# Six sorted tiles of a graph layer are routed one or two steps later

## The reference, cut to what matters

```python
edge_index = jnp.stack([src, dst])
xn = _layernorm(x, axis=-1)
x = x + gnn(xn, edge_index, ...) + mix(xn[None], ...)[0]   # attention over edges; token mixing
x = x + ffn(_layernorm(x, axis=-1)[None], ...)[0]          # 8 experts, best 2 per node
```

## Time and profile before

| what | us |
|---|---|
| median of 3 runs (2192.88 to 2195.23) | 2193.44 |
| the profiled execution | 2191.56 |
| its span | 2189.8 |
| busy: PE, DVE, POOL, ACT | 1831.5, 1600.6, 1454.8, 1085.2 |

### The profile page before, as it was taken

One profiled execution on the slowest core, in us unless ns is written; L12 is line 12 of the kernel. 1 busy time (PEld: TensorE's weight loads), 2 busy tenths in 40 slices (PEclk: granted clock), 3 DMA queues, 4 the chain that ended last, 5 costly groups with the idle time before them and its releaser, 6 DMA issues. The chain is left out here.

```text
span 2189.8 us, 37617 instructions
## 1 busy us (share of the span) xinstructions
PE 1831.5 (84%) x9074; PEld 1332.9 (61%) x9075; DVE 1600.6 (73%) x3942; ACT 1085.2 (50%) x1932; POOL 1454.8 (66%) x1586
## 2 busy tenths in 40 slices
PE   8499998687777787775789999889999989997871
PEld 6367776566556565554566667667767777764540
DVE  7588887568677777697777888879878989731143
ACT  4333333236454555355556667667647767632210
POOL 3277777777777777775567777667777777700376
PEclk9799999888777877877999999999999999999985
DMA  9666565876666666655567777666778777622485
GB/s 331 140 191 180 170 173 147 263 218 193 167 176 175 182 175 184 177 143 152 161 186 208 210 207 217 190 179 192 194 195 210 213 208 181 166 68 70 145 248 161
DMA packets 287067, 402.19 MB, mean 184 GB/s; under 512 B 108915, under 2 KB 209555, under 8 KB 283262
## 3 DMA queue, kind: packets, MB, share of 16 engines
q0 software_dynamic: 74208, 206.08, 35.0%
q1 hardware_dynamic: 197036, 180.03, 27.5%
q10 hardware_dynamic: 15602, 13.59, 2.1%
HBM read 346.38 MB, written 82.48 MB: 196 GB/s over the span
## 5 line engine op out<-in xcount | busy, mean ns | idle before, releaser
L1546 POOL DMA_INDIRECT rows_g<-node_table,src_all x1347 | 1281.6, 951 | 506.5 <-issue 409.5
L2336 PE MATMUL psB<-rows_g,pick_e 128*128 128x260 f32 x2704 | 737.4, 433 | 138.7 <-issue 116.0
L2336 PEld LDWEIGHTS psB<-rows_g,pick_e 128*128 128x128 f32 x2704 | 576.6, 219 | 257.2 <-issue 155.0
L1721 DVE TENSOR_TENSOR rows_g<-rows_g,psD 128x2048 f32<-128x2048 f32 x169 | 384.9, 2277 | 0.0
L2134 ACT ACTIVATE pick_n<-local_row 128x1024 bf16<-128x1024 bf16 x169 | 178.6, 1057 | 214.1 <-PE psA L2325 203.5
L2377 PE MATMUL psC<-W_f,xnT 128*128 x448 | 225.8, 627 | 0.0
L1568 POOL DMA_INDIRECT rows_g<-set_dram,places x98 | 96.8, 988 | 168.5 <-issue 164.2
L1692 DVE TENSOR_TENSOR pick_e<-psD,slot_all 128x1024 f32<-128x1024 f32 x169 | 203.7, 1205 | 0.1
L2130 ACT ACTIVATE local_row<-local_row,minus_id 128x1024 bf16<-128x1024 bf16 x169 | 191.5, 1133 | 15.8 <-DVE both_f L2034 8.7
L1784 DVE COPY xn<-psD 128x256 f32<-128x256 f32 x112 | 47.2, 421 | 180.7 <-PE psD L2413 75.9
L2325 PEld LDWEIGHTS psA<-window,pick_n 128*128 128x128 bf16 x1352 | 54.2, 98 | 150.0 <-issue 145.5
(11 more groups left out here) (389 smaller groups left out, 3013.3 us busy)
## 6 DMA issues: line engine op xcount, KB each, us to landing
local_row<-local_dram SPq DMA_DIRECT2D x169, 256.0 KB
sent_dram<-sorted_dram SPq DMA_DIRECT2D x176, 128.0 KB
rows_g<-node_table,src_all POOLq DMA_INDIRECT x1347
xin<-sent_dram SPq DMA_DIRECT2D x112, 128.0 KB
set_dram<-xn SPq DMA_DIRECT2D x112, 128.0 KB
xnT<-in_xT_dram SPq DMA_DIRECT2D x96, 128.0 KB
acc<-node_table SPq DMA_DIRECT2D x49, 128.0 KB, 3.6
W_f<-in_x_dram SPq DMA_DIRECT2D x48, 128.0 KB, 2.9
```

What stands on the lines that cost most here:

```text
L1546: pool.indirect_dma_start(out=rows_g[:, r, j], out_offset=None, in_=node_table, in_offset=bass.IndirectOffsetOnAxis(ap=src_all[:, g, j:j + ...
L1721: dve.tensor_tensor(heads, heads, p_here.unsqueeze(3).broadcast_to([P, EG, HEADS, C]), ALU.mult).then_inc(ph_ready, 1)
L2336: last = pe.matmul(ps_sum[s % 2][:, 0:AW], pick_e[:, s % SLOTS, j], rows_g[:, s % RING, j, 0:AW], start=(j == 0), stop=(j == EG - 1))
```

## The change

```diff
         if t + 3 <= FULL:
-            at = max(at, route_at[t + 3] + (4 if t + 3 >= CUTS[0] else 5))
+            at = max(at, route_at[t + 3] + (4 if t + 3 >= CUTS[0] else 6))
+        if t + 2 < CUTS[0]:
+            at = max(at, route_at[t + 2] + 3)
```

## The result

Measured beside the kernel before, the changed kernel took 2166.32 us (median of 4 runs, 2165.59 to 2171.48) against 2193.16: the ratio is 0.9887, with a 95% interval of 0.9875 to 0.9899. That is 24.8 us less by the ratio and 26.8 by the medians. The prediction was 2173.8 us, 19.6 less. The span of the profiled execution went from 2189.8 to 2165.1 us.

A forecast was written before the change was run, and what follows sets the result against it. It took DVE's waits on PE's sorting product to hold up steps 82 to 89, and PE to bound steps from 94 on. -29.3 + 2 + 3.7 + 4 = -19.6 us gave 2173.8 us, range 2164 to 2182.

The forecast's parts named there:

- What bounds which steps: PE bounds steps 94 to 107; in steps 82 to 89 (112.9 us) neither PE nor DVE is always busy, something is serial.
- The five waits: DVE's waits on PE's sorting product in steps 82, 83, 84, 87 and 88, together 29.3 us, were to go.
- They are worth 29.3 us: Removing DVE's five waits on the sorting product was entered in the sum as 29.3 us less.
- (a) Step 82: DVE's `choose(21)` needs logits that PE forms late in step 81; 2 us given back, bounds 0 and 5.0.
- (b) Work moved past step 93: Three sorting-product halves of tiles 17 and 16 move to PE-bound steps 94 and 95; 3.7 us given back.
- (c) PE as the cover: In steps 82 to 93, without DVE's waits, steps must be long enough for PE; 4 us given back, at most 13.5.
- The clock rule: PE's clock dips thin out once long gaps go; the skill page would have them stay with the short gaps.
- All of it: Rival, chance 0.07: none of (a) to (c) shows in steps 82 to 93; 29.3 us less, 2160 to 2164 us.
- PE takes over: Rival, chance 0.18: DVE waits for PE's end of step instead; 7.1 us less, about 2186 us.
- The slower case: Rival, chance 0.05: PE falls to half clock for most of steps 82 to 93; at 0.65, 15 us slower, 2208 us.

The follow-up runs named there:

- e3: Kernel before with its own steps, plus four buffers of normalised rows for sorted tiles and three homes of the selection matrix; saved 14.1 us, ratio 0.9932.
- e2: Changed kernel with five instead of six steps behind the third tile ahead (routes 78, 80, 81, 83, 85, 86); saved 18.8 us, ratio 0.9914.
- e9: Kernel before with e3's buffers and only tile 21's route moved, from 77 to 78; saved 17.4 us, ratio 0.9926.
- e5: e3's buffers with e2's steps, against the kernel before; saved 28.0 us, ratio 0.9872.
- e1: Changed kernel without its rule of three steps behind the second tile ahead (routes 77, 81, 82, 83, 87, 88); saved 14.9 us, ratio 0.9923.
- e7: Kernel before with 46 extra unread PE products, in step 81 and at the start of steps 83, 84 and 88; ratio 1.0001.
- e6: Changed kernel with seven steps behind the third tile ahead instead of six, four behind the second instead of three; saved 7.4 us, ratio 0.9962.
- e12: Changed kernel with a ring of four buffers of normalised rows (`xd`) for every tile; ratio 0.9892.
- e4: Changed kernel with seven instead of six steps behind the third tile ahead; saved 28.1 us, ratio 0.9867.

## Why the prediction was right or wrong, point by point

**What bounds which steps.** Right. Steps 82 to 89 held the loss (112.9 us, now 90.5), and from step 94 on PE passes on what it gets (147.9 and 147.6 us for steps 94 to 107). Steps 82 to 93 take 133.8 us, within the 123 to 140 that were foretold.

**The five waits are gone.** Right: 29.3 us to 0.

**They are worth 29.3 us.** This step failed as a reason, and that its sum came out near is in part luck. By e3, taking away these waits and nothing else is worth 14.1 us, because PE's long steps then hold DVE up at the logits instead. The saving follows the fall of all of DVE's waits on PE in steps 80 to 93, whatever they wait for. From 31.3 us before they fall by 16.5 in e3, 19.1 in e2, 20.1 in e9, 23.3 in the change and 29.3 in e5, which save 14.1, 18.8, 17.4, 26.8 and 28.0; the match is loosest in e1, where they fall by 9.8 and 14.9 are saved. The prediction asked of each `normed` and `sort_out` where its product stood, but not how long PE's list was in that step, nor what else waited for its end. The change takes three things away together: the same-step waits (worth 9.2 us once nothing is three-deep, e5 against e2), the three-deep steps with ACT's wait for the store (13.9 us once there are no such waits, e5 against e3), and some half clock. Each masks part of the other: both alone come to 18.8 and 14.1, and together to 28.0, not 32.9. What the three-deep step, the store and the clock are worth each by itself stays open.

**(a) Step 82.** 2 us was put down; the wait on the logits of tile 21 is there, in step 82, and takes 0.98 us.

**(b) Work moved past step 93.** 3.7 us was put down for three products in steps 94 and 95. What is given back shows in PE's time: PE's sums of step 92 and of step 96 after the change (starts; a row counts the matmuls up to the end of the stretch asked for),

```profile
1112.81 1.48 PE L2338 MATMUL psB<-rows_g,pick_e 128*128 128x260 f32 x6
...
1124.63 5.31 PE L2338 MATMUL psB<-rows_g,pick_e 128*128 128x260 f32 x16 [1.42 <-DVE rows_g L1723]
...
1158.59 1.77 PE L2338 MATMUL psB<-rows_g,pick_e 128*128 128x260 f32 x7 [1.23 <-issue]
```

start 28.7 us ahead of before in step 92 (1141.52) and 24.3 us ahead in step 96, where the kernel before has

```profile
1182.91 1.33 PE L2336 MATMUL psB<-rows_g,pick_e 128*128 128x260 f32 x5 [1.42 <-DVE rows_g L1721]
```

So 4.4 us were given back, near the term's size, but for other reasons in the main. The lead of PE's sums falls by 1.1 us in step 92, by 1.6 in step 93, whose own sums take 5.31 us (3.67 before), by 1.5 in step 94 and by 0.1 in step 95. The products that moved past step 93 cost some 1.7 us, not 3.7; the rest is the slower sums of step 93 and the 1.1 us in step 92. By the starts of the steps, 94 and 95 together are 2.5 us shorter than before (24.3 against 26.8), where the prediction had looked for 2 to 4 us more.

**(c) PE as the cover.** 4 us was put down. In the prediction's own sum this is the mis-sized term: at step 92 PE is 28.7 us ahead, and 29.3 less that leaves 0.6 us for (a) and (c) together. New waits on the logits did come (3.07 us in step 85, 1.44 in step 86), near the term's size. But steps 82 to 93 run at 0.96 instead of 0.88 and 1.00, and no step is three-deep, which the sum did not count. The prediction named steps 84 and 90 as those without a `sort_out`; by the table of `route_at` steps 82, 85, 88 and 91 have none either, and the longest new wait stands in 85. The sum was short by 5.2 us: 24.8 were measured by the ratio.

**The clock rule.** The Trainium skill, "TensorE: Matmul & The Clock Gate", "A second HAM failure mode: psum-queue depth-cycling", tells of a kernel in which short idle times between groups of matmuls made the clock swing between its two levels. By that the dips would have stayed with the gaps of 1.4 us. They thinned out, from 0.88 to 0.96 in steps 82 to 89, as forecast. But the rows don't speak against the page, as the prediction had it, because the short gaps did not stay. Ahead of the sums of steps 82 to 89 PE stood for 1.3 us or more seven times before (1.34 to 1.92 us), and twice after (1.48 and 1.42). Of steps 90 to 93 before, which the prediction took as its example, only 91 and 92 have such a gap. Nor is it so that every step with a standstill shows a low clock: of the five, 82 and 87 show 0.94 and 1.00.

What the traces show agrees with the page: in steps 82 to 107 of the fourteen kernels profiled, 42 of 364 groups of sums took over 5 us instead of 3.7, and each of the 42 came behind a gap of 0.5 us or more (one of them is the row of step 93 above). Such a gap is not enough by itself: 125 groups came behind a gap of over 1 us, and 85 of them took 3.7 us. In e7, with the long gaps filled for the most part and the waits kept, the dips went to other sums.

**The rivals.** "All of it" (29.3 us or more) comes as near as the forecast or nearer (4.5 us off by the ratio, where the forecast is 5.2 off), but what it asked for, that none of (a) to (c) shows, is not what happened. "PE takes over" did not happen in the change, and is what happened in e3 and e6. The slower case needed a mean clock below 0.71; steps 82 to 93 ran at 0.96. The gain was handed on to the end whole: 24.3 us at step 96, 24.7 in the span.

## What to carry to other kernels

When an engine waits for another in the same step of a hand-made schedule, the wait's length is the other engine's list up to that point; before costing its removal, write down for each step what every engine has in it, and ask what else waits for the end of the longest list. A buffer that removes a wait without shortening that list moves the wait: here 29.3 us of waits were worth 14. And taking away a wait gains nothing while another engine's issues already fill the step, as GpSimd's did in e12: count those issues per 200 us first.

## What the runs showed that was not expected

Moving two tiles by one step each was worth 13.9 us (e3 to e5), and one step in three tiles cost 20.7 us (e4 to e6), though the work was the same. A ring of two on ACT and SP, which no wait of the kernel before showed, held ACT up for 3.4 us as soon as PE came early. And 46 extra products of 128 columns (9.5 us more of PE's busy time) did not change the time by more than the noise, in either direction.
